# Setup of a two-block AdaLN kernel, taken apart and spread over the queues and engines

## What is computed

```
mod = (silu(c) @ wmod).reshape(32, 6, 1, 128)        # sa, ca, ga, sb, cb, gb; per layer
ga, gb = sign * max(|.|, 0.25)                       # the two gates are clamped
x = x + ga * attention(layernorm(x) * (1 + ca) + sa)
x = x + gb * ffn(layernorm(x) * (1 + cb) + sb)
```

## Time and profile before

| | us |
|---|---|
| median of 3 runs (1906.49 to 1907.74) | 1906.71 |
| the profiled execution, own time | 1907.06 |
| its span, first to last instruction | 1905.3 |
| PE, DVE busy in the span | 1699.7, 1678.0 |
| ACT, POOL busy in the span | 716.5, 68.9 |

### The profile page before, as it was taken

One profiled execution on the slowest core, in us unless ns is written; L12 is line 12 of the kernel. 1 busy time (PEld: TensorE's weight loads), 2 busy tenths in 40 slices (PEclk: granted clock), 3 DMA queues, 4 the chain that ended last, 5 costly groups with the idle time before them and its releaser, 6 DMA issues.

```text
span 1905.3 us, 37018 instructions
## 1 busy us (share of the span) xinstructions
PE 1699.7 (89%) x12297; PEld 1317.1 (69%) x12297; DVE 1678.0 (88%) x3791; ACT 716.5 (38%) x1447; POOL 68.9 (4%) x78
## 2 busy tenths in 40 slices
PE   2347799999999999999999999999999999999998
PEld 1234567776776767677686767777676777768787
DVE  5578799989899998989989998999989899997775
ACT  0122435262533426253432526243352525334332
POOL 0000000000000000000000000000000000000000
PEclk7686899999999999999999999999999999999999
DMA  4020302003030301203030110303021030303000
GB/s 142 25 76 28 109 5 89 28 20 98 5 107 10 104 14 27 86 15 97 10 105 13 50 63 18 99 5 106 12 63 51 18 99 6 100 10 91 12 13 8
DMA packets 130106, 97.25 MB, mean 51 GB/s; under 512 B 28000, under 2 KB 124512, under 8 KB 125824
## 3 DMA queue, kind: packets, MB, share of 16 engines
q1 hardware_dynamic: 121536, 91.74, 16.4%
q10 hardware_dynamic: 8448, 4.20, 0.7%
HBM read 56.48 MB, written 29.98 MB: 45 GB/s over the span
## 4 chain that ended last, share of the span: by engine, by line
PE 47%; DVE 37%; issue 9%; ACT 4%; SPq 1%; DVEq 1%; DMA 1%; POOL 0%; ACTq 0%; POOLq 0%
DVE mneg L1099 9%; PE y_ps L1476 9%; PE bank L1469 5%; PE bank L1471 5%; PE bank L1470 5%; DVE h L1196 4%; PE bank L1220 4%; DVE tt L1188 3%; PE bank L1436 3%; ACT arena L770 2%; DVE xh L967 2%; PE bank L1343 2%; DVE arena L1107 2%; PE bank L1373 2%; PE bank L1420 2%
## 5 line engine op out<-in xcount | busy, mean ns | idle before, releaser
L813 ACT ACTIVATE tt<-bank 128x512 f32<-128x512 f32 x352 | 212.4, 603 | 665.8 <-PE bank L1471 523.9
L1476 PEld LDWEIGHTS y_ps<-wd,h 128*128 128x128 f32 (+1 forms) x3072 | 379.1, 192 | 70.7 <-issue 19.1
L1476 PE MATMUL y_ps<-wd,h 128*128 128x128 f32 (+1 forms) x3072 | 415.4, 282 | 14.1 <-DVE h L1196 14.1
L1196 DVE TENSOR_TENSOR h<-tt,bank 128x512 f32<-128x512 f32 x352 | 236.0, 682 | 23.6 <-PE bank L1471 7.1
L1188 DVE SCALAR_TENSOR_TENSOR tt<-tt,bank 128x512 f32<-128x512 f32 x352 | 237.2, 682 | 21.4 <-ACT tt L813 14.7
L1099 DVE TENSOR_REDUCE mneg<-bank 128x2 f32<-128x512 f32 (+1 forms) x384 | 236.0, 680 | 3.9 <-issue 2.4
L770 ACT ACTIVATE arena<-bank 128x512 f32<-128x512 f32 x384 | 196.5, 612 | 34.8 <-PE bank L1417 20.7
L1469 PE MATMUL bank<-h_hi,wg_hi 128*128 128x512 f32 x352 | 164.2, 466 | 10.3 <-DVE h_lo L1163 3.8
L1469 PE MATMUL bank<-h_hi,wu_hi 128*128 128x512 f32 x352 | 163.1, 463 | 8.4 <-DVE mneg L1099 8.3
L1107 DVE TENSOR_TENSOR arena<-arena,keep_k 128x1024 f32<-128x1024 f32 (+1 forms) x96 | 149.0, 1577 | 20.4 <-ACT arena L770 18.8
L1471 PE MATMUL bank<-h_lo,wg_hi 128*128 128x512 f32 x352 | 140.5, 399 | 0.0
(11 more groups left out here) (183 smaller groups left out, 2647.0 us busy)
## 6 DMA issues: line engine op xcount, KB each, us to landing
q_stack<-q_rows SPq DMA_DIRECT2D x16, 1024.0 KB, 4.8
k_stack<-k_rows SPq DMA_DIRECT2D x16, 1024.0 KB, 8.0
q_rows<-qk_halves SPq DMA_DIRECT2D x48, 256.0 KB, 2.8
k_rows<-qk_halves SPq DMA_DIRECT2D x48, 256.0 KB, 2.9
rows<-mod_rows SPq DMA_DIRECT2D x48, 128.0 KB, 3.0
rows<-mod_rows SPq DMA_DIRECT2D x16, 384.0 KB, 3.5
x_in<-in_L_attn_X SPq DMA_DIRECT2D x16, 256.0 KB, 2.8
vals<-arena SPq DMA_DIRECT2D x128, 32.0 KB, 5.2
```

The source lines that it names most:

```text
L813: send(a(tt[:, ch % 2, :], ps.bank(f"eg{ch}")[:], ACT.Tanh, scale=0.5), tanh_ready)
L1196: frees(v.tensor_tensor(h32[:, ch % 3], tt[:, ch % 2, :], ps.bank(f"eu{ch}")[:], ALU.mult), f"eu{ch}")
L1476: ins = mm(y_ps[:, P * t:P * (t + 1)], h32[rows_, ch % 3, P * t:P * (t + 1)], wd[rows_, ch, :], start=first and t == 0, stop=last_ and t = ...
```

## The change

1. c goes into `mixed` instead of `x_in`, and c and `wmod` get a semaphore of their own, `s_cond` (4 loads). ACT's tanh waits for these four alone. `s_ld` keeps the other 11.
2. The 31 loads of FP4 weights, w1, w3 and w2 move from SP's stream to ACT's. They stand between the tanh and the copy of `sct`.
3. SP's first `load1` no longer waits for DVE's rows: the load of the first pair comes ahead of that wait. The store of `mod_rows` and its wait stand inside the first `load1`, ahead of `rows1`.
4. DVE makes silu(c) ahead of `wl_s`, gives out its credits ahead of the modulation, and clamps in three wide calls instead of eight.
5. Quantising leaves the setup: gate and up are quantised behind the first pair's `norm1`, down behind its `quantise_x` 2. PE turns the three weights through `y_ps` behind the first pair's `scores0` 1, `out0` and `turn2`, and ACT copies them out behind its `scores0` 1, `probs0` 1 and `turn2`.
6. The splits of w1 and w3 move from DVE to POOL: the first behind the first pair's `stats1`, the second behind its `stats2`.
7. PE waits for weights where it first needs them (`first_pair` conditions in `down0`, `gate`, `up`, `down`).
8. Staging areas in the arena move to other places; the first pair's tiles of layer 0 no longer overlap them.

The core of the diff:

```diff
-        def turns(eng, order, mine):
+        def turns(eng, order, mine, follow={}):
...
-                        mine[name](Turn(reg, plus + lead), *which)
+                        it = Turn(reg, plus + lead)
+                        mine[name](it, *which)
+                        if first_pair(it) and (name, *which) in follow:
+                            follow[(name, *which)]()
...  sync
-            sp.dma_start(x_in[0:NB, 0, :], c0).then_inc(s_ld, 16)
-            sp.dma_start(x_in[0:NB, 1, :], c1).then_inc(s_ld, 16)
-            sp.dma_start(wmod_s[0], wmod0).then_inc(s_ld, 16)
-            sp.dma_start(wmod_s[1], wmod1).then_inc(s_ld, 16)
+            sp.dma_start(mixed[0:NB, 0, :], c0).then_inc(s_cond, 16)
+            sp.dma_start(mixed[0:NB, 1, :], c1).then_inc(s_cond, 16)
+            sp.dma_start(wmod_s[0], wmod0).then_inc(s_cond, 16)
+            sp.dma_start(wmod_s[1], wmod1).then_inc(s_cond, 16)
...
+                if first_pair(it):
+                    sp.wait_ge(s_rows_ready, 1)
+                    sp.dma_start(mod_rows, row_tile).then_inc(s_rows, 16)
+                    sp.wait_ge(s_rows, 16)
                 send(sp.dma_start(rows1[:], rows_from(it, 0, 1)), rows1_loaded)
...  gpsimd
+            def split(src, hi, lo, n):
+                pool.wait_ge(s_w[n], 16 * 8)
+                g.tensor_copy(hi[:], src).then_inc(s_split, 1)
+                pool.wait_ge(s_split, n + 1)
+                g.tensor_tensor(lo[:], src, hi[:].bitcast(F32), ALU.subtract).then_inc(s_ready, 1)
...  scalar
-            act.wait_ge(s_ld, 16 * SMALL)
-            a(res[0:NB, 0:2, :], x_in[0:NB, 0:2, :], ACT.Tanh, scale=0.5).then_inc(s_act0, 1)
+            act.wait_ge(s_cond, 16 * 4)
+            a(res[0:NB, 0:2, :], mixed[0:NB, 0:2, :], ACT.Tanh, scale=0.5).then_inc(s_act0, 1)
+            act.wait_ge(s_zero, 1)
+            for n, w in enumerate((w_gate, w_up)):
+                for c, (c_at, c_n) in enumerate(FCH):
+                    act.dma_start(fp4_in[0:c_n, 3 * n + c, :], w[c_at:c_at + c_n, :]).then_inc(s_fp4, 16)
+            act.dma_start(fp4_down, w_down).then_inc(s_fp4, 16)
...
+            for e in range(EXP):
+                columns(stage[0], w1, e, s_w[0])
+            for e in range(EXP):
+                columns(stage[1], w3, e, s_w[1])
...
             act.wait_ge(s_ct, 1)
             a(sct, y_ps[:, 0:2 * NB], ACT.Copy).then_inc(s_sct, 1)
...
+            def fp4_gate():
+                act.wait_ge(s_fp4t, 1)
+                a(wgt_s[:], y_ps[:, 0:FI], ACT.Copy).then_inc(s_fp4c, 1)
...  vector
-            for j in (2, 5, 8, 11):
-                clamp(modt[:, j, :], modt[:, j, :], res[:, 0, 0:NB], res[:, 1, 0:NB])
+            gates = modt[:, 2:12:3, :]
+            clamp(gates, gates, *[res[:, n, 0:4 * NB].rearrange("p (j b) -> p j b", b=NB) for n in range(2)])
...
+            def fp4_halves():
+                dve.wait_ge(s_fp4, 16 * 7)
+                for half in range(2):
+                    part_ = fp4_in.rearrange("p c k -> p (c k)")[:, 3 * P * half:3 * P * (half + 1)]
+                    block_scales(step0, part_, 3 * P // QB)
+                    to_grid(step0, part_, fp4_w1, fp4_w2, 3 * P // QB)
+                    step0(rounded(step0, part_, fp4_w1, fp4_w2, 3 * P // QB))
+                    dve.sem_inc(s_fp4q, 1)
...  the follow maps of pool, scalar, vector and tensor, in this order
+{("stats1",): lambda: split(stage[0], wg_hi, wg_lo, 0), ("stats2",): lambda: split(stage[1], wu_hi, wu_lo, 1)}
+{("scores0", 1): fp4_gate, ("probs0", 1): fp4_up, ("turn2",): fp4_down_}
+{("norm1",): fp4_halves, ("quantise_x", 2): fp4_third}
+{("scores0", 1): lambda: fp4_turn(0), ("out0",): lambda: fp4_turn(1), ("turn2",): lambda: fp4_turn(2)}
```

More of the change, by code:

```diff
@@ L311, in adaln_two_blocks @@
         h3t, v32 = part(15808, TOK), part(16320, TOK)
[L313 to L317, removed]
+        stage = [part(6592, CHUNKS, P), part(9664, CHUNKS, P)]
+        fp4_in, fp4_down = part(12736, 6, P), part(13504, FI)
+        fp4_w1, fp4_w2 = part(13856, 6 * P), part(14624, 6 * P)
+        wmod_s = [part(2048, 6 * P), part(2816, 6 * P)]
+        qkv_s = part(3584, 3 * P)
         vals = sb("vals", [P, 32, 2 * NHP])
@@ L430, in send, with first_pair @@
             ins.then_inc(s.sem, s.step)
-        def turns(eng, order, mine):
+        def first_pair(it):
+            return it.reg is None and it.plus == 0
+        def turns(eng, order, mine, follow={}):
             def turn(reg, plus):
@@ L646, in stats4 @@
                 root(it, n3, var3_ready, rstd3_ready, 1)
-            turns(pool, pool_order, dict(stats1=stats1, stats2=stats2, stats3=stats3, stats4=stats4))
+            def split(src, hi, lo, n):
[3 more added lines that the diff above has]
+                g.tensor_tensor(lo[:], src, hi[:].bitcast(F32), ALU.subtract).then_inc(s_ready, 1)
+            turns(pool, pool_order, dict(stats1=stats1, stats2=stats2, stats3=stats3, stats4=stats4), {("stats1",): lambda: split(stage[0], wg_hi, wg_lo, 0), ("stats2",): lambda: split(stage[1], wu_hi, wu_lo, 1)})
         @block.scalar
@@ L821, in _ @@
                             turn_max=turn_max, rows=rows, weigh=weigh, turn_att=turn_att, turn4=turn4, logits=logits,
-                            halves4=halves4, gate=gate, finish=finish))
+                            halves4=halves4, gate=gate, finish=finish), {("scores0", 1): fp4_gate, ("probs0", 1): fp4_up, ("turn2",): fp4_down_})
             act.wait_ge(stored.sem, 16 * (PAIRS + 1))
@@ L887, in _ @@
             step0(v.tensor_copy(ident_b[:], ident[:]))
+            dve.wait_ge(s_act0, 1)
+            step0(v.scalar_tensor_tensor(tmp2[0:NB, 0:2, :], res[0:NB, 0:2, :], 1.0, mixed[0:NB, 0:2, :], ALU.add, ALU.mult))
+            v.tensor_scalar(tmp2[0:NB, 0:2, :], tmp2[0:NB, 0:2, :], 0.5, None, ALU.mult).then_inc(s_silu, 1)
             dve.wait_ge(s_ld, 16 * SMALL)
@@ L892, in _ @@
             step0(last)
[L894 to L896 removed]
+            credits(dve, x1_ready, x2_ready, x3_ready, begun, y_free, gated, out_ready)
             dve.wait_ge(s_mod, 1)
@@ L1211, in _ @@
                             stats4=stats4, swish=swish, times=times, mix=mix,
-                            finish=finish))
+                            finish=finish), {("norm1",): fp4_halves, ("quantise_x", 2): fp4_third})
         @block.tensor
@@ L1233, in _ @@
             mm(pool_banks[2][0:NB, P:2 * P], sct[:, NB:2 * NB], wmod_s[1][:, 5 * P:6 * P], start=True, stop=True).then_inc(s_mod, 1)
[L1234 to L1243 removed]
+            pe.wait_ge(s_ld, 16 * SMALL)
             credits(pe, down_done)
@@ L1505, in finish, with fp4_turn @@
                 down(it, CHUNKS - 1)
+            def fp4_turn(n):
+                pe.wait_ge(s_fp4q, n + 1)
+                if n:
+                    pe.wait_ge(s_fp4c, n)
+                for c, (c_at, c_n) in enumerate(FCH):
+                    if n < 2:
+                        last = turn(y_ps[:, c_at:c_at + c_n], fp4_in[0:c_n, 3 * n + c, :], c_n)
+                    else:
+                        last = turn(y_ps[0:c_n, P * c:P * (c + 1)], fp4_down[:, c_at:c_at + c_n])
+                last.then_inc(s_fp4t, 1)
             turns(pe, pe_order, dict(turn1=turn1, query0=query0, key0=key0, value0=value0, scores0=scores0, probs0=probs0, out0=out0,
@@ L1510, in _ @@
                            turn_out=turn_out, turn_att=turn_att, turn4=turn4, logits=logits, gate=gate, up=up, down=down,
-                           finish=finish))
+                           finish=finish), {("scores0", 1): lambda: fp4_turn(0), ("out0",): lambda: fp4_turn(1), ("turn2",): lambda: fp4_turn(2)})
         for s in signals:
```

101 lines of the change are left out of this document (38 added, 63 removed).

## The result

| | before | after |
|---|---|---|
| median of 6 runs each, us | 1907.20 (1904.16 to 1908.11) | 1937.81 (1931.60 to 1941.57) |
| profiled execution, own time; span, us | 1907.06; 1905.3 | 1941.57; 1939.5 |

The ratio after to before is 1.0163, with a 95% interval of 1.0145 to 1.0181. The change is 1.6% slower. The prediction was 1910.6, with 1916 as the upper end of its range. That has the sign, but an eighth of the loss.

A forecast was written before the change was run, and what follows sets the result against it. PE and DVE were taken to share the bound, with a serial setup behind DVE. An earlier first pair gained 17.8 - 0.6 - 3.1 = 14.1 us, POOL's splits cost 18.0: +3.9, forecast 1910.6 us, range 1890 to 1916.

The forecast's parts named there:

- the last stretch: Behind 240 us: PE busy 1575 of 1665 us, DVE 1512, and nothing of the change touches it.
- third effect: PE at the lower clock for long behind 60 us, put at 1 us.
- Tanh: Setup, ACT: waits for four loads only and ends at 6.45 us, 3.9 earlier than before.
- 31 issues on ACT: Setup, between tanh and `sct` copy: issues last until 23.7 us, bounds 18.3 to 26.9, making `sct` 11.7 later.
- PE's products and the clamps: Setup behind `sct`: 8.34 us to `modt`, then adds and clamps 7.1 instead of 11.3, statistics at 39.3.
- Splits on POOL: Splits of w1 and w3 in pair 0: 9.0 us each, bounds 5.0 to 12.4.
- Exclusion: Pair 0's `norm1` and `norm2`: DVE's SBUF work and POOL's splits block each other, price 18.0 us, chance 0.62.
- rivals A and B: POOL beside DVE: first, no hindrance, 1892.6, chance 0.22; second, only the subtraction excludes, 1903.4, chance 0.10.
- The price on pair 0's path: Pair 0 behind its statistics: 18.0 us for blocked DVE and PE's clock, 0.6 and 3.1 for turning and quantising weights.
- the first turn: Ahead of pair 0's `probs0`: three transposes of nine and an ACT copy cost 0.6 us.
- the third: Down weights quantised behind `quantise_x` 2: 4.2 us of DVE, first gate product at 95.1, 3.1 us lost.
- Rival C: Setup: ACT's issues don't hold up the copy of `sct`, 11.7 us more gained, 1898.9 or 1880.9, chance 0.06.

The follow-up runs named there:

- a_pad28: The changed kernel with 28 already satisfied waits added on DVE, 792 instructions ahead of its loop: 1918.08 us, ratio to before 1.0052.
- a_pad208: The changed kernel with 208 already satisfied waits added on DVE, 972 instructions ahead of its loop: 1914.77 us, ratio to before 1.0058.
- a_pad240: The changed kernel with 240 already satisfied waits added on DVE, 1004 instructions ahead of its loop: 1913.82 us, ratio to before 1.0053.
- a_pad16: The changed kernel with 16 already satisfied waits added on DVE, 780 instructions ahead of its loop: 1912.60 us, ratio to before 1.0037.
- experiment 12: The changed kernel with 792 DVE instructions ahead of the loop and ACT's copy of `sct` ahead of its 31 issues: 1891.98 us, ratio to before 0.9939.
- experiment 11: The changed kernel with 792 DVE instructions ahead of the loop and both splits run by DVE at the same places: 1905.37 us, ratio to before 0.9999.

## Why the prediction was wrong, step by step

**The step that failed** is the sentence on the last stretch: PE is busy 1575 of 1665 us there "and nothing of the change touches it". The change touches it through the number of DVE instructions ahead of the loop. That put a term of 21 to 27 us into every comparison of a dear with a cheap start. Next to it, everything else in my sum was small. I named PE at the lower clock for long behind 60 us as a possible third effect and put it at 1 us in all. In the turn shown it takes 1.5 of the 2.6 us lost, and there are ten such turns; a DVE pause of one microsecond stands ahead of each.

**The rest, with the jump made cheap.** Against the predicted ratio of 1.0020 three cheap paddings of after (a_pad28, a_pad208, a_pad240) measure 1.0052 to 1.0058, and a_pad16 measures 1.0037. In the profiles the root at 217 us is 6.0 late in after and 6.5 to 7.0 in a_pad16 and a_pad28.

- *Tanh.* Ends at 6.55, predicted 6.45. Right.
- *31 issues on ACT.* Predicted to 23.7, range 18.3 to 26.9. They ended at 27.2, just outside. This is the one mis-sized term of the setup, 3.5 us. Five issues between 9.4 and 15.3 us took 0.69 to 1.67 us each. SP's own issues ended at 11.44, ahead of the two longest, so the 1.1 us that I had counted for the two streams getting in each other's way do not explain all of it; what held these issues is not shown. The mechanism, `sct` behind the queue, was right (experiment 12).
- *PE's products and the clamps.* 8.34 and 7.2 us, both as predicted. The statistics came at 42.84 instead of 39.3, and the root is 14.3 ahead of before instead of 17.8.
- *Splits on POOL.* 8.64 us each, 2.53 and 6.11, predicted 9.0. Exclusion was the case bet on, and experiment 11 shows it from the other side. It begins with POOL's copy, not only with its subtraction, so rivals A and B are out.
- *The price on pair 0's path.* Predicted 18.0 for exclusion (1.0 of them PE's clock), 0.6 for the first turn and 3.1 for the third, 21.7 in all. The starts against before (and `norm2` above) divide what was measured up to the first gate product. `norm1` starts 14.3 us early and `smax` (64.01) 6.1 early, so 8.2 went there. `norm2` starts 5.3 early (76.72 against 82.03), so the first turn and PE's clock cost 0.8 together. `norm2` lasts 9.24 instead of 1.11, 8.1 more. The first gate product comes 4.9 us behind the end of `quantise_x` (92.84) instead of 1.9, so the third costs 3.0. The sum is 20.1, and the gate product (97.77 against 91.98) is 5.8 late.
- *Rival C,* the issues not holding `sct`, is out.

So the mechanisms of the local sum were right. The issues were 3.5 us too cheap in it and the path 1.6 too dear: 3.9 + 3.5 - 1.6 = 5.8. The cheap starts measure +7 to +11, and the 1 to 5 us between are not traced. The rest of the distance to the measured +31 is the jump.

## What to carry to other kernels

An edit to the setup of a looped kernel changes where each engine's loop starts. Before a small difference is believed, look at the first instruction behind the jump in each turn for a wait on "issue", look for two instruction fetches close together just ahead of it, and run the kernel once with some idle instructions ahead of the loop. A few microseconds in a setup can come out at the end in full when the first item's pieces hand over one by one, so what stands in one engine's queue ahead of a small copy that all others wait for is the first thing to move. Work moved to GpSimd beside VectorE's SBUF work isn't free: here it cost VectorE 8.1 us to be spared 4.7.

## What the runs showed of the hardware that was not expected

- **The start of DVE's loop.** With 764, 768 or 1020 instructions ahead of it, each jump back costs 1.2 to 1.4 us of DVE (10.7 to 12.5 us in nine). With 780, 792, 832, 872, 972 or 1004 it costs 0.2 to 0.4. In the dear kernels two instruction fetches start within 0.7 us of each other just ahead of the jump, in the cheap ones never within 4.7. If the place repeats, as 764 and 1020 suggest, it does so in 256 or 128. Whether the loops of the other engines have the same is not shown; no run moved one of them alone.
- **A pause of PE costs more than itself.** After 1.76 us of idling the granted clock was 0.54 for the next 3.7 us, after 0.64 us it stayed at 1.00. That added 1.5 us to a wait that was 1.1 us longer. Ten of ten such jumps had it in after, two of ten in before, one of these behind a pause of 0.66 us.
- **GpSimd on large f32 tiles.** A copy of 128x2816 took 2.53 us and a subtraction 6.11, against DVE's 1.62 and 3.09. Each held one DVE normalise of 0.33 us until it was through itself, 2.53 and 6.27 us. The Trainium skill, page SBUF — State Buffer, section Who interferes with whom, gives the exclusion as a rule, and this trace agrees. DVE's first instruction got through between GpSimd's two: it ended at 48.15, 0.08 us behind the copy, and the second was held by the subtraction.
- **DMA issues on two queues.** ACT's issues took 0.69 to 1.67 us each from 9.4 to 15.3 us, and 0.45 to 0.46 in the 6 us behind. SP's issues beside them (two stores of constant rows, the first pair's load) ended at 11.44. SP alone had 0.52 on average for the same 31. What stretched ACT's is not shown.
